# Two message-passing layers with expert mixtures: the first mixture's residual additions, the norm behind it and the edge projection of the nodes put into one block, in three groups of tiles

## What is computed

```python
x = x + gnn0(ln(x)) + mix0(ln(x))
t = ln(x)
x = x + moe(t)
xn = ln(x)
x = x + gnn1(xn, edges) + mix1(xn)
x = x + ffn1(ln(x))

def moe(t):
    out = t
    for e in range(8):
        h = gelu(t @ w1[e] + b1[e])
        out = out + combine[:, e:e+1] * (h @ w2[e] + b2[e])
    return out

def gnn1(h, edges):
    hid = relu((h[src] + edge_attr) @ W1 + b1)
    msg = hid @ W2 + b2
    return h + segment_sum(msg, dst)
```

## Time and profile before

| | us |
|---|---|
| three runs | 1331.40, 1331.01, 1337.01 (median 1331.4) |
| the profiled execution's own time | 1334.28 |
| its span, first to last instruction | 1332.3 |
| PE busy | 1123.4 (84%) |
| VectorE busy | 662.3 (50%) |
| ScalarE busy | 440.5 (33%) |
| GpSimd busy | 485.2 (36%) |
| mean granted TensorE clock | 0.937 of full |

### The profile page before, as it was taken

The page is one execution under the profiler, slowest core; times in us unless marked ns, Lnnn a source line. Parts: engine busy times, 40 slices in busy tenths (PEclk is TensorE's granted clock), DMA queues, the critical chain, the costliest instruction groups (busy, mean ns, idle before and its releaser), DMA issues. The chain is left out here.

```text
span 1332.3 us, 21998 instructions
## 1 busy us (share of the span) xinstructions
PE 1123.4 (84%) x7698; PEld 907.6 (68%) x7698; DVE 662.3 (50%) x1616; ACT 440.5 (33%) x923; POOL 485.2 (36%) x530
## 2 busy tenths in 40 slices
PE   2888898998538884379999999999999799938997
PEld 2688897466427773268788888888876645527886
DVE  5777731678664323735454555554375512152332
ACT  2477710522315441113243333333333242321110
POOL 3000000103026773027766666666574000004442
PEclk9899999998859997589999999999999889968998
DMA  6000000500352334556566666666573094386551
GB/s 134 1 2 2 2 2 16 109 4 1 102 172 90 101 100 116 140 162 197 183 192 184 186 190 186 190 190 179 161 220 105 14 305 105 82 201 211 180 182 38
DMA packets 97268, 164.52 MB, mean 123 GB/s; under 512 B 15633, under 2 KB 59309, under 8 KB 96901
## 3 DMA queue, kind: packets, MB, share of 16 engines
q1 hardware_dynamic: 71669, 89.65, 23.4%
q0 software_dynamic: 25488, 73.39, 18.9%
HBM read 137.36 MB, written 27.63 MB: 124 GB/s over the span
## 5 line engine op out<-in xcount | busy, mean ns | idle before, releaser
L2357 POOL DMA_INDIRECT em_gathered<-edge_table,el_which x313 | 301.4, 963 | 131.2 <-issue 74.8
L2369 PE MATMUL em_projected<-em_w,em_attr 128*128 128x256 f32 x1252 | 281.3, 382 | 7.6 <-PEq L1988 7.6
L2369 PEld LDWEIGHTS em_projected<-em_w,em_attr 128*128 128x128 f32 x1252 | 238.8, 191 | 42.3 <-issue 9.9
L2447 DVE TENSOR_TENSOR em_hidden<-em_projected,em_gathered 128x512 f32<-128x512 f32 (+1 forms) x157 | 108.2, 689 | 204.0 <-PE em_projected L2369 125.1
L2469 ACT ACTIVATE em_hidden<-em_hidden 128x512 f32<-128x512 f32 (+1 forms) x157 | 98.7, 628 | 270.2 <-DVE em_hidden L2447 269.6
L2869 PE MATMUL oe_banks<-oe_wd,xn_T 128*128 x432 | 99.1, 384 | 0.0
L2783 POOL DMA_INDIRECT oe_hidden<-oe_table,oo_node x27 | 25.9, 960 | 182.1 <-DMA oe_table<-state 131.3
L2869 PEld LDWEIGHTS oe_banks<-oe_wd,xn_T 128*128 128x128 f32 x432 | 81.3, 193 | 10.2
L2812 PE MATMUL oe_banks<-xn_T,oe_w 128*128 128x500 f32 x160 | 71.1, 596 | 1.8 <-DMA oe_b<-in_ffn_b_T 1.8
L663 ACT ACTIVATE nm_adj_T<-nm_banks 125x500 f16<-125x500 f32 x100 | 60.0, 603 | 23.0 <-PE nm_banks L566 19.9
L1380 POOL IOTA el_up_i<- 20x40 int32 x1 | 0.2, 161 | 180.1 <-POOLq L741 180.1
(11 more groups left out here) (502 smaller groups left out, 2218.9 us busy)
## 6 DMA issues: line engine op xcount, KB each, us to landing
em_attr<-in_edge_attr_sets SPq DMA_DIRECT2D x156, 256.0 KB, 3.5
oe_table<-state SPq DMA_DIRECT2D x20, 448.0 KB
oe_wd<-in_ffn_Wd SPq DMA_DIRECT2D x8, 1024.0 KB
em_gathered<-edge_table,el_which POOLq DMA_INDIRECT x313, 3.6
mx_w<-in_ffn_w SPq DMA_DIRECT2D x16, 256.0 KB
oe_table<-state SPq DMA_DIRECT2D x1, 2248.8 KB
state<-in_x SPq DMA_DIRECT2D x5, 448.0 KB
state<-in_x SPq DMA_DIRECT2D x1, 2240.0 KB
```

Of the source, the lines that this page charges most:

```text
L2357: nc.gpsimd.indirect_dma_start(out=gathered[:, n % GATHERED, :], out_offset=None, in_=table, in_offset=bass.IndirectOffsetOnAxis(ap=lanes. ...
L2369: last = nc.tensor.matmul(projected[:, k % BANKS, n % 2, :], attr[:, k % ATTR_RING, (n % 2 * KB + f) * 128:(n % 2 * KB + f + 1) * 128], w1 ...
L2447: nc.vector.tensor_tensor(pair_slots(k), projected[:, k % BANKS, 0:width, :], gathered[:, at:at + width, :], ALU.add).then_inc(pre_ready, 1)
```

## The change

The additions, the norm and the projection move into the block of `mixture`, which gets a tail in three groups of tiles: 0 to 7, 8 to 15 and 16 to 19. `normalise_to_first` is gone, and with it one meeting of all engines.

* VectorE adds and measures the tiles of a group, finds their variance (`find_var`), adds the first tile of the next group, and only then inverts the root of the group before (`find_root`), which now also gives `shift`, the negative mean times the inverse root.
* ScalarE takes the root, normalises (`activation` with `Identity`, `scale=std`, `bias=shift`, both one column), copies the transposed tile and also moves the product out of PSUM. Its list holds a whole group before the next group's root.
* PE waits for all expert results, then transposes and projects by groups. The bias is now a third matmul for each tile, of one row of ones by one row of the bias.
* SP loads the eight pairs of edge features and the five weights right after the mixture's own weights, during the routing. The table's chunks go out from the space of the experts' weights (`staged`). `edge_messages` starts with SP clearing 52 semaphores, and GpSimd there waits for the stored table before its first gather; the block of `mixture` does not wait for it.
* To find the SBUF space, `rows` and `hidden_T` of the mixture lie in `answer`, and two tables of the routing (`hot_row`, `values`) lie in `w1_now` and `rows_T`.

```diff
-def mixture(p, c, A, state, x, xn, xn_T, first_w, first_b):
+def mixture(p, c, A, state, x, xn, xn_T, first_w, first_b, edge):
...
+        GROUPS, BANKS = ((0, 2), (2, 4), (4, CHUNKS)), 4
+        tiles_in = lambda g: range(4 * GROUPS[g][0], 4 * GROUPS[g][1])
...
             def _(sp):
...
                 clear(sp, done)
+                for k in range(ATTR_RING):
+                    load_attributes(sp, A, edge.attr, edge.attr_loaded, k)
+                edge.weights.sync(sp)
                 for u in range(RESULTS):
                     sp.wait_ge(written[u], len(range(u, TILED, RESULTS)) * 16)
...
+                for q in range(CHUNKS):
+                    sp.wait_ge(kept, 4 * (q + 1))
+                    load_rows(sp, edge.table[q * CHUNK:(q + 1) * CHUNK, :].rearrange("(t p) d -> p t d", p=P), staged(q), edge.stored)
...
+                def project(t):
+                    pe.wait_ge(copied, t + 1)
+                    if t >= BANKS:
+                        pe.wait_ge(kept, t - BANKS + 1)
+                    for k in range(KB):
+                        nc.tensor.matmul(projected[:, t % BANKS, 0:DIM], xn_T[:, k, t * P:(t + 1) * P], first_w[:, k, :],
+                                         start=(k == 0), stop=False)
+                    nc.tensor.matmul(projected[:, t % BANKS, 0:DIM], c.ones[0:1, 0:P], first_b[0:1, :],
+                                     start=False, stop=True).then_inc(ready, 1)
...
+                for g in range(len(GROUPS)):
+                    for t in tiles_in(g):
+                        turn_rows(t)
+                        if t - 2 in tiles_in(g):
+                            project(t - 2)
+                    for t in tiles_in(g)[-2:]:
+                        project(t)
...
+                for g in range(len(GROUPS)):
+                    mine = slice(tiles_in(g)[0], tiles_in(g)[-1] + 1)
+                    act.wait_ge(var_ready, g + 1)
+                    nc.scalar.activation(std[:, mine], var[:, mine], ACT.Sqrt).then_inc(std_ready, 1)
+                    act.wait_ge(rooted, g + 1)
+                    for t in tiles_in(g):
+                        nc.scalar.activation(xn[:, t, 0:DIM], x[:, t, :], ACT.Identity, bias=shift[:, t:t + 1],
+                                             scale=std[:, t:t + 1]).then_inc(normed, 1)
+                        if t - 1 in tiles_in(g):
+                            keep_turned(t - 1)
+                        if t - 3 in tiles_in(g):
+                            keep_rows(t - 3)
+                    keep_turned(tiles_in(g)[-1])
+                    for t in tiles_in(g)[-3:]:
+                        keep_rows(t)
...
+                for g in range(len(GROUPS)):
+                    for t in tiles_in(g):
+                        add_answers(t)
+                        if t - 1 in tiles_in(g):
+                            measure(t - 1)
+                        if g and t == tiles_in(g)[0]:
+                            find_root(g - 1)
+                    measure(tiles_in(g)[-1])
+                    find_var(g)
+                find_root(len(GROUPS) - 1)
...
-def normalise_to_first(p, c, A, x, xn, xn_T, w, b, attr, attr_loaded, table, others, done):
...
             def _(sp):
+                clear(sp, done)
                 for k in range(ATTR_RING, PAIRS):
...
                 nc.gpsimd.iota(order_i[:], [[1, P]], base=0, channel_multiplier=0).then_inc(numbered, 1)
+                pool.wait_ge(edge.stored, 32 * CHUNKS)
                 for n in range(BLOCKS):
```

More of the change, by code:

```diff
@@ L1606, with __init__ @@
 class Origins:
-    def __init__(self, p, scope, name, top, tiles):
+    def __init__(self, p, scope, name, top, tiles, hot_row=None, values=None):
         self.nc, self.top, self.tiles = p.nc, top, tiles
@@ L1753, in mixture @@
         answered = [[sem(f"answered{n}_{q}") for q in range(CHUNKS)] for n in range(TOP)]
-        added = sem("added")
+        added, measured = sem("added"), sem("measured")
+        GROUPS, BANKS = ((0, 2), (2, 4), (4, CHUNKS)), 4
+        tiles_in = lambda g: range(4 * GROUPS[g][0], 4 * GROUPS[g][1])
+        mean, var, half, std, shift = (sb(n, [P, TILES]) for n in ("mean", "var", "half", "std", "shift"))
+        w2 = sb("w2", [128, EXPERTS * KB * DIM])
+        w1 = sb("w1", [128, EXPERTS * KB * DIM])
+        norm_turned, projected = banks[:, 0:BANKS], banks[:P, BANKS:2 * BANKS]
+        staged = lambda q: (w1[:P, q * 4 * DIM:(q + 1) * 4 * DIM] if q < 4 else w2[:P, EXPERTS * KB * DIM - 4 * DIM:]).rearrange("p (t d) -> p t d", d=DIM)
+        s6 = c.stats[:].rearrange("p (t k) -> p k t", k=6)
+        var_ready, std_ready, rooted, normed = sem("var_ready"), sem("std_ready"), sem("rooted"), sem("normed")
+        transposed, copied, ready, kept = sem("transposed"), sem("copied"), sem("ready"), sem("kept")
         by_block = lambda a: a.rearrange("(k p) n -> p k n", p=128)
@@ L1948, in measure, with add_answers @@
                     dve.wait_ge(added, (t + 1) * TOP)
-                    nc.vector.bn_stats(c.stats[:, t * 6:(t + 1) * 6], x[:, t, :])
-                for t in range(TILES):
+                    nc.vector.bn_stats(c.stats[:, t * 6:(t + 1) * 6], x[:, t, :]).then_inc(measured, 1)
+                def add_answers(t):
                     for n in range(TOP):
@@ L1968, in load_attributes @@
     sp.dma_start(attr[:, k % ATTR_RING, 0:2 * DIM if s < SETS - 1 else DIM], source).then_inc(attr_loaded[k % ATTR_RING], 16)
-def normalise_to_first(p, c, A, x, xn, xn_T, w, b, attr, attr_loaded, table, others, done):
[L1974 to L2042, removed]
-                        last = nc.tensor.transpose(turned[:, t % BANKS, k * P:(k + 1) * P],
-                                                   xn[:, t, k * 128:(k + 1) * 128], c.ident[:P, :P])
-                    last.then_inc(transposed, 1)
[L2046 to L2049, removed]
-            @block.scalar
-            def _(act):
-                act.wait_ge(var_ready, 1)
-                nc.scalar.activation(std[:], var[:], ACT.Sqrt).then_inc(std_ready, 1)
-                for t in range(TILES):
-                    act.wait_ge(transposed, t + 1)
-                    nc.scalar.activation(xn_T[:, :, t * P:(t + 1) * P],
-                                         turned[:, t % BANKS, 0:KB * P].rearrange("p (k n) -> p k n", k=KB),
-                                         ACT.Copy).then_inc(copied, 1)
@@ L2357, in _ @@
                     nc.gpsimd.indirect_dma_start(
-                        out=gathered[:, n % GATHERED, :], out_offset=None, in_=table, in_offset=bass.IndirectOffsetOnAxis(
+                        out=gathered[:, n % GATHERED, :], out_offset=None, in_=edge.table, in_offset=bass.IndirectOffsetOnAxis(
                             ap=lanes.which[:, n:n + 1].bitcast(mybir.dt.uint32), axis=0)).then_inc(got[n % GATHERED], 16)
@@ L2653, in __init__ @@
         self.b2, self.gamma = p.sb("em_b2", [P, DIM], scope=scope), p.sb("at_gamma", [P, DIM], scope=scope)
-        self.loaded = p.sem("at_loaded")
+        self.loaded = p.sem("at_loaded", False)
     def sync(self, sp):
```

86 lines of the change are left out of this document (60 added, 26 removed).

## The result

| | before | after |
|---|---|---|
| median of four runs each, us | 1331.67 | 1368.03 (1365.0 to 1370.27) |
| span of the profiled execution, us | 1332.3 | 1368.4 |
| mean granted TensorE clock | 0.937 | 0.919 |

The ratio is 1.0262, with an interval of 1.0226 to 1.0299: slower by 2.6%, and outside the range of the prediction, whose upper end was 1337.5.

The account below looks back on a forecast made before the run. VectorE's additions, PE's projections and a closing piece lay in a row, with PE bounding the new tail. First gather 3.6 us earlier, less 2.1 for one clock fall, gained 1.5: 1329.9 us from 1331.4, range 1319.5 to 1337.5.

Parts of the forecast that it names:

- PE for a tile: Tail's projection: the bias matmul adds 0.43 us (0 to 0.87), so a tile takes 1.51 us, 8.7 us more over 20 tiles.
- At full from there on: PE's clock in the projection before: half at first, full after 5.6 us of work; assumed for group one's start.
- the clock does not come back: Rival: clock falls in the first gap, stays half through groups two and three, 16.9 us more, 1344.7 us; chance 0.10.
- my cases: None, one or two clock falls in the gaps between groups: 1327.8 to 1332.0 us, 1329.9 with one; chance 0.58 together.
- Both gaps: Clock between groups: one fall taken, 2.1 us lost for each; the rival with both falling gives 1332.0, within the 0.58.
- A gap: Between groups, projection to projection: 4.2 us, as ScalarE's next root stands in its list behind the last product.
- ScalarE's normalising: ScalarE's work for a tile in the tail: 0.55 us taken, between 0.38 and 0.79, with PE still setting the pace.
- The closing piece: Tail's end to the first gather: last product at 581.75, block start 582.85, gather 584.75 against 588.35, 3.6 us gained.
- The gathers: Edge block's start: PE's wait at 605.38 hangs on the gathers, so the gain is how much earlier the first goes out.
- The rival of PE's start: Edge block: the wait has another cause, and an earlier start with PE warm gains 7.0 us, 1324.4; chance 0.16.
- The early loads: Loads during routing: 3.7 MB, 10 us, costed at nothing; rival that they delay the mixture's gathers, 4 us, 1333.9, chance 0.08.
- True overlap: Rival in the tail: ScalarE's order does not hold the roots, VectorE is the bound, 17.7 us gained, 1313.7; chance 0.08.

Follow-up runs that it names:

- e2: The kernel of e1 with the third matmul, and so the bias of the edge table, left out: 1324.08 us, ratio 0.9943.
- e1: The changed kernel with the bias matmul of 125 rows (identity by the bias in all rows) in place of one row: 1332.14 us, ratio 0.9997.
- b1: The kernel before with the bias as a one-row matmul in its projection loop, VectorE only copying: 1379.16 us, one of four runs 1347.51 us.
- e3: The kernel of e1 with one pipeline over the group borders, the next root taken before the last products are moved: ratio 0.9916 and, on another chip, 0.9924.
- e5: The kernel of e1 with one group of 20 tiles in place of three: 1339.14 us, ratio 1.0042.
- e9: The kernel of e1 with a one-row matmul of 16 columns added behind the 125-row bias matmul: 1425.91 us on a slower chip, ratio 1.0052.
- e4: The kernel of e3 without the third matmul, the bias added in SBUF by GpSimd in 20 additions: ratio 0.998.

## Why the prediction was wrong

**The step that failed** is the bias in "PE for a tile": "I take 0.43, since a matmul's time in the rows goes with its columns", with 0.87 at half clock as its upper bound. For 125 rows that holds (e2: 0.40 to 0.53, e1: a tile of 1.52 against 1.51). For one row two things break it. The load of its weights does not overlap with its neighbours, 0.44 us a tile at half clock beyond the time of the columns; and while such matmuls of 256 columns run, the clock does not come back, but for one run of b1. The rows of before could not have told. They hold matmuls of few rows, 20 transposes of 8 rows in the routing, but these follow one another without a stop and are over in 2.25 us:

```profile
357.61 2.25 PEld L1860 LDWEIGHTS mx_banks<-ident,mx_answer 8*125 8x125 f32 x20 [0.82 <-ACT mx_answer L1879]
```

"At full from there on", after 5.6 us, was taken from a stretch with 125 and 128 rows and carried over to work of another shape. A tile took 3.46 us where I had 1.51.

The sum of it, an estimate: after has 20 x 3.46 = 69.2 us of tiles. e1 has 20 x 1.52 = 30.4, and three starts at half clock, 2.1 us each by the prediction's estimate, 6.3. The difference is 32.5, and the distances of after and e1 differ by 33.6.

**The rival that came true** was "the clock does not come back", with a chance of 0.10 and 1344.7 us. Its mechanism was named and its price too small: it let the clock come back in group one and fall in a gap, so counted 16.9 us. In the trace all three groups ran at half clock, and the stops came on top. It also blamed the gaps, and b1 has none.

**What held**, by e1, which is the change as I had costed it: 0.9 us below the kernel before (1332.14 against 1333.07, and the interval of the ratio holds 1), where my cases gave between 0.6 more and 3.6 less than 1331.4.
* Both gaps let the clock fall, not one: the Trainium skill's rule on bursts ("TensorE: Matmul & The Clock Gate", HAM oscillation) held in e1's stretches at 560 and 580, with clocks of 0.83 and 0.85, and e3, which keeps the work together, gains 10 us. With both falls my distance is 68.4 - 3.6 + 4.2 = 69.0, and e1 has 68.3.
* A gap was 4.2 us by the count and 4.35 in after; in e1, at full clock ahead of it, the first is 4.10 (from 558.79 to 562.89). ScalarE's list holds the root back, as said.
* ScalarE's normalising was 0.55 by my choice and 0.591 measured; the Trainium skill ("ScalarE: Activation LUTs", What ACT_TABLE_LOAD costs) gave an estimate of 585 ns, and the trace agrees.
* The closing piece gained less: from the end of the last product's move it was 588.35 - 580.50 = 7.85 us before, I had 584.75 - 581.75 = 3.0, and it was 626.38 - 622.68 = 3.70. That is a gain of 4.15 in place of 4.85.
* The gathers set the start of the edge block: PE's wait for ScalarE grew from 0.43 to 2.28 us. And in e1 PE starts the edge block 66.0 us behind the first load of answers, against 67.7 before, and its first 16 records take 3.69 us, against 5.68; the first gather comes only 0.1 us earlier, and the kernel is no faster than that. The rival of PE's start falls.
* The early loads did not delay the mixture. Its first gather came 4.2 us later than before, but the shift is that of the first answers above: e5, with the early loads, has this gather at 389.06, and b1, without them, at 393.5.
* True overlap was rightly left out: ScalarE's order held the roots.

## What to carry to other kernels

A bias as a one-row matmul is not free, nor is it priced by its columns: here it cost a weight load that does not overlap, and with it TensorE's clock stayed at half for 80 us. With the identity and the bias in all rows the same product cost 0.40 us. Before carrying "the clock comes back after so much work" to new code, look whether the new work has the same number of rows; and if a pipeline is cut into groups, let the next group's head start before the last products of the old one are moved. Work given to an idle engine can cost more at the end of a block than it saves inside it: look how long that engine takes from its last instruction to the next block.

## What was not expected of the hardware

* Matmuls with 1, 32 and 64 rows had the same median duration, 707 to 709 ns at half clock, against 634 for 128 rows, and each left the weight load idle for 0.65 us on both sides. With one row and 16 columns at full clock it is 0.33 ahead and 0.03 behind (e9).
* TensorE, busy for 20 of 20 us by the profile, stayed at half clock (after, 580 to 600). With 256 columns and 1, 32 or 64 rows in the third matmul the clock stayed low in every trace; with 16 columns and one row it came back, with a stop ahead of each one-row load.
* A block whose last instructions are GpSimd's additions ended late: 8.03 us from the end of the last one to the next block (e4), against 1.8 us that PE stands at the same place in after. And VectorE's additions took 0.93 to 0.98 us while GpSimd added, in place of 0.47 to 0.49.
